# A graph network of four layers: two node stages and the attention layer's edge loop rewritten

## The reference, cut to what matters

```python
h = relu(layernorm(x)); x = x + schnet(h)     # node part: h @ w1.T goes into a table of nodes
h = relu(layernorm(x)); x = x + gat(h)        # attention layer
h = relu(layernorm(x)); x = x + mean(h)       # mean layer
h = relu(layernorm(x)); x = x + gcn(h)        # begins with h @ W1, 256 -> 64

def gat_conv(x, ...):
    h = (x @ W.T).reshape(n, 8, 32)
    logits = leaky_relu(a_s[src] + a_d[dst])
    m = segment_max(logits, dst)
    e = exp(logits - m[dst])
    return segment_sum(e / segment_sum(e, dst)[dst] * h[src], dst)

def mean(x, ...):
    return segment_sum((x @ W + b)[src], dst) / degree
```

## Time and profile before

| what | us |
|---|---|
| three runs | 5814.14, 5817.79, 5822.13 |
| median | 5817.79 |
| profiled execution | 5819.96 |
| its span, first to last instruction | 5818.2 |
| embedding | about 9 to 123 |
| attention layer's edges | about 1694 to 2965 |
| closing stage of the mean layer | about 4203 to 4337 |

### The profile page before, as it was taken

The page is one execution under the profiler, slowest core; times in us unless marked ns, Lnnn a source line. Parts: engine busy times, 40 slices in busy tenths (PEclk is TensorE's granted clock), DMA queues, the critical chain, the costliest instruction groups (busy, mean ns, idle before and its releaser), DMA issues. The chain is left out here.

```text
span 5818.2 us, 87770 instructions
## 1 busy us (share of the span) xinstructions
PE 4193.3 (72%) x24069; PEld 3457.8 (59%) x24069; DVE 3748.1 (64%) x8398; ACT 1534.4 (26%) x2511; POOL 3534.6 (61%) x3559
## 2 busy tenths in 40 slices
PE   4999999999869888888866555555563333333793
PEld 3888888888658888888855555555543333333231
DVE  4999999999548888888875444444453333333673
ACT  3766666676221111111123000000020000000570
POOL 1677777776037777777702777777627777777003
PEclk8999999999978888888887777777785555555796
DMA  5433333333334444444434333333331111111243
GB/s 164 128 102 104 103 105 103 104 103 96 95 102 110 107 107 104 106 103 102 103 106 123 105 105 105 105 105 105 108 102 32 27 27 27 27 27 27 72 113 104
DMA packets 417658, 538.48 MB, mean 93 GB/s; under 512 B 200349, under 2 KB 289577, under 8 KB 417353
## 3 DMA queue, kind: packets, MB, share of 16 engines
q0 software_dynamic: 154912, 381.74, 24.1%
q1 hardware_dynamic: 262442, 152.99, 9.8%
HBM read 482.43 MB, written 58.81 MB: 93 GB/s over the span
## 5 line engine op out<-in xcount | busy, mean ns | idle before, releaser
L1881 POOL DMA_INDIRECT l_rows<-tmp_tab,src_sb x1664 | 1576.8, 948 | 517.9 <-issue 496.3
L1994 PE MATMUL l_psa<-l_sel,l_rows 128*128 128x128 f32 (+1 forms) x4992 | 998.3, 376 | 1076.9 <-DVE l_sel L1893 819.7
L1994 PEld LDWEIGHTS l_psa<-l_sel,l_rows 128*128 128x128 f32 (+1 forms) x4992 | 878.5, 248 | 1197.5 <-DVE l_sel L1893 908.3
L1907 DVE TENSOR_TENSOR acc<-acc,l_psa 128x256 f32 (+1 forms) x1664 | 583.8, 351 | 1242.8 <-PE l_psa L1994 1076.1
L495 POOL DMA_INDIRECT l_rows<-tmp_tab,l_idx x832 | 883.7, 1062 | 373.4 <-issue 252.0
L1159 POOL DMA_INDIRECT l_rows<-tmp_tab,l_idx x832 | 891.8, 1072 | 297.3 <-issue 219.8
L793 PE MATMUL l_psw<-l_fw,l_ssp 128*128 128x256 f32 x3328 | 763.1, 382 | 0.0
L793 PEld LDWEIGHTS l_psw<-l_fw,l_ssp 128*128 128x128 f32 x3328 | 615.9, 190 | 153.7 <-issue 77.3
L1473 PE MATMUL l_psa<-l_sel,l_rows 128*128 128x128 f32 x3328 | 597.8, 308 | 33.7 <-DVE acc L1361 26.4
L1361 DVE TENSOR_TENSOR acc<-acc,l_psa 128x384 f32 x832 | 460.5, 554 | 169.2 <-issue 67.6
L1473 PEld LDWEIGHTS l_psa<-l_sel,l_rows 128*128 128x128 f32 x3328 | 501.8, 216 | 59.5 <-DVE acc L1361 36.2
(11 more groups left out here) (311 smaller groups left out, 5711.4 us busy)
## 6 DMA issues: line engine op xcount, KB each, us to landing
l_rows<-tmp_tab,l_idx POOLq DMA_INDIRECT x1664
l_edge<-in_edge_t SPq DMA_DIRECT2D x104, 256.0 KB
l_rows<-tmp_tab,src_sb POOLq DMA_INDIRECT x1664
tmp_x<-n_X SPq DMA_DIRECT2D x39, 512.0 KB
n_X<-in_x SPq DMA_DIRECT2D x26, 512.0 KB
tmp_tab<-n_O POOLq DMA_DIRECT2D x26, 512.0 KB
l_win<-tmp_att_tab SPq DMA_DIRECT2D x832, 8.0 KB
n_X<-tmp_x SPq DMA_DIRECT2D x26, 512.0 KB
```

Of the source, the lines that this page charges most:

```text
L1881: nc.gpsimd.indirect_dma_start(out=rows[g % ROWS][:, t, :], out_offset=None, in_=table[:, :], in_offset=bass.IndirectOffsetOnAxis(ap=sh["s ...
L1907: nc.vector.tensor_tensor(a, a, p, ALU.add).then_inc(added, 1)
L1994: last = nc.tensor.matmul(by_tile(g)[0:n, t, k * P:(k + 1) * P], rows[b][:, t, f:f + n], sel[b][:, t, :], start=True, stop=True)
```

## The change

In the embedding ScalarE applies the ReLU of chunk n - 1 before it copies out chunk n - 2.

In the attention layer's edges the column numbers are copied once to PSUM (`iota_ps`), and `select` reads them there. ScalarE takes the exponential of the differences twice, into `wx` for TensorE and into a PSUM area `w_ps` for VectorE; both areas share the PSUM tile `fixed`. `val_ps` moves from a tile of its own to the end of `psm`. VectorE waits for the weights ahead of the fourth select. GpSimd takes its indices straight from the tile of source numbers, with no copies, no loop and no wait for `val_done`.

The closing stage of the mean layer is new. PSUM is one tile of four quarters, and a chunk keeps one quarter: TensorE transposes the aggregate into it from `acc` directly, then the norm, the product of 64 columns, and at last the transposed table. ScalarE normalizes with a scale and a shift, VectorE makes the shift. The product with features along the partitions and its scaling are gone: the scaled table `O` is transposed (`flip`) and ScalarE copies it to `acc3` (`own_columns`). Four chunks of x are held.

```diff
@@ embed0, ScalarE
                     if at(0):
                         nm.deviations(act, at(0))
+                    if at(1):
+                        nm.relu(act, at(1), mm_done)
                     if at(2):
                         copy_out(nc, act, ph, O, psO, at(2), mm_done, stored, o_done)
-                    if at(1):
-                        nm.relu(act, at(1), mm_done)
@@ edges_gat
-        val_ps, att_ps = ph.ps("val_ps", 512)[:, 0:SH], ph.ps("att_ps", 512)[:, 0:SH]
+        att_ps = ph.ps("att_ps", 512)[:, 0:SH]
         psm = ph.ps("psm", 512)
+        val_ps = psm[:, 512 - SH:512]
+        fixed = ph.ps("fixed", 512)
+        iota_ps, w_ps = fixed[:, 0:P], fixed[:, P:P + SH]
...
+                                in_offset=bass.IndirectOffsetOnAxis(ap=sh["src_sb"][:, n * SEG + j:n * SEG + j + 1].bitcast(U32),
+                                                                    axis=0),
...
                     nc.scalar.activation(by_edge(wx[c.p])[:, :, 0:HEADS], diff[c.p][:, :].rearrange("p (t h) -> p t h", h=HEADS),
-                                         ACT.Exp).then_inc(w_done, 1)
+                                         ACT.Exp)
+                    nc.scalar.activation(w_ps, diff[c.p][:, :], ACT.Exp).then_inc(w_done, 1)
...
+                    nc.vector.tensor_tensor(sel[c.p][:, b * GT:(b + 1) * GT, :], iota_ps.unsqueeze(1).to_broadcast([P, GT, P]),
+                                            col.unsqueeze(2).to_broadcast([P, GT, P]), ALU.is_equal).then_inc(sel_done, 1)
...
+                    w = w_ps.rearrange("p (t h) -> p t h", h=HEADS)[:, part, :]
+                    nc.vector.tensor_tensor(m, m, w.unsqueeze(3).to_broadcast([P, GT, HEADS, HID]),
...
                     if a:
                         add(a, 3)
+                    if m:
+                        dve.wait_ge(w_done, m.n + 1)
                     if c:
                         select(c, 3)
@@ nodes_mean, new
+    DEEP = 4
+        ps = ph.ps("psU", DEEP * CT * D)
+        psU = [ps[:, r * CT * D:(r + 1) * CT * D] for r in range(DEEP)]
...
+        def unrolled(step):
+            for s in range(CHUNKS + 3):
+                step(*(s - j if 0 <= s - j < CHUNKS else None for j in range(4)))
...
+                for n in range(CHUNKS):
                     sp.wait_ge(x_done, n + 1)
+                    sp.dma_start(node_rows(dram["x3"], n), X[n % DEEP][:, :, :]).then_inc(x_stored[n % DEEP], 16)
+                    if n + DEEP - 1 < CHUNKS:
+                        load(n + DEEP - 1)
...
+                def own_columns(n):
+                    act.wait_ge(flipped, n + 1)
+                    nc.scalar.activation(acc3[:, n * CN:(n + 1) * CN], psU[n % DEEP][0:H3, CN:2 * CN], ACT.Copy).then_inc(copied, 1)
+                def normalize(n):
+                    act.wait_ge(shift_done, n + 1)
+                    after(act, xT_done, n - 1)
+                    for t in range(CT):
+                        last = nc.scalar.activation(norm[n % 2][:, t, :], X[n % DEEP][:, t, :], ACT.Identity,
+                                                    bias=shift[n % 2][:, t:t + 1], scale=rstd[n % 2][:, t:t + 1])
@@ nodes_mean, ScalarE
+                def step(new, mid, old, last):
+                    if old is not None:
+                        relu(old)
+                    if mid is not None:
+                        normalize(mid)
+                    if last is not None:
+                        own_columns(last)
+                    if new is not None:
+                        deviations(new)
@@ nodes_mean, VectorE
+                def step(new, mid, old, last):
+                    if mid is not None:
+                        shifts(mid)
+                    if new is not None:
+                        residual(new)
+                    if old is not None:
+                        table(old)
...
+                def back(n):
+                    after(pe, copied, n - DEEP + 1)
...
+                def flip(n):
+                    pe.wait_ge(o_done, n + 1)
+                    for t in range(CT):
+                        last = nc.tensor.transpose(psU[n % DEEP][0:H3, CN + t * P:CN + (t + 1) * P], O[n % 2][:, t, :],
+                                                   sh["ident"][:, :])
+                    last.then_inc(flipped, 1)
@@ nodes_mean, TensorE
+                def step(new, mid, old, last):
+                    if old is not None:
+                        turn(old)
+                    if new is not None:
+                        back(new)
+                    if last is not None:
+                        flip(last)
+                    if old is not None:
+                        product(old)
```

186 lines of the change are left out of this document (90 added, 96 removed).

## The result

Three runs took 5731.73, 5733.31 and 5735.03 us, median 5733.31, against 5817.79 before: 84.5 us less, a ratio of 0.9855 (0.9836 to 0.9875). The forecast was 5748, 72 less, and the range ended at 5735. So the direction and each part's sign held, and the forecast gain was too small in all three terms.

A forecast was written before the change was run, and what follows sets the result against it. Barriers make the time the sum of stages, each bound by its own limiting chain. Savings of 15.5 (embedding), 53.4 (closing stage) and 3 (attention edges), 72 us, from 5820.0 give 5748; range 5735 to 5770.

The forecast's parts named there:

- 4.60 in all: Embedding: TensorE sets the new turn, 3.56 us to the transposes plus 1.04 for them, instead of 5.99.
- 1.5 for the low clock: Closing stage of the mean layer: early turns may run at the low clock and add 1.5 us.
- the 0.3 a turn for work that doesn't mesh: Closing stage: engine sums up to 4.5 us don't mesh for nothing, so turns were taken as 4.8 us.
- Rival (b): Closing stage doesn't mesh, 6.0 us a turn, from transfers or low clock: 14 us less gain, 5762; 12 in 100.
- The steps on queues and transfers: Closing stage: loads have three turns, 14 us, to land; 246 GB/s fits under 317 at a full share.
- The median of the selects as the price of a PSUM operand: Attention edges: select from PSUM 680 ns against 684, 0.8 us less over 208; no difference taken for messages.
- The Trainium skill's figure: VectorE access overhead about 60 ns for SBUF, 125 for PSUM: 65 ns on 416 instructions, 27 us.
- The 2 us for GpSimd's relief in the fill: Attention edges: earlier start, two copies fewer and no stretched gathers bring the second chunk's values 2.0 us earlier.
- rival (c): Attention edges: VectorE's 67.1 us of issue gaps halve as GpSimd stops competing for the port: 5714; 5 in 100.
- (a): Attention edges: PSUM operands cost 34 ns on 416 VectorE instructions, so the 3 us don't come: 5765; 8 in 100.
- (d): Attention edges: banks shared by three engines make VectorE wait, slower than before; 0.25 us per instruction gives 5852; 2 in 100.
- The embedding's end of 17: Embedding: upper end of the saving, forecast at 15.5 us with ends of 11 and 17.

The follow-up runs named there:

- h3: Kernel before with GpSimd's direct gathers, message weights from PSUM with the second exponential, and VectorE's earlier wait; select still from SBUF: 5808.8 us, ratio 0.9994.
- j2: Kernel of h3 with VectorE's wait for the weights left ahead of the first message: 5814.3 us, ratio 1.0001 against the kernel before.
- g1_sel: Kernel before with GpSimd's direct gathers and the select's column numbers in PSUM, message from SBUF: 6647.6 us against 6570.7 on the slow chip, ratio 1.0104.

## Why the prediction missed by two microseconds

**The base.** 5748 is counted from the profiled execution's 5820.0. From the median, 5817.8, the same gains give 5745.9, and the same range would end at 5732.8. So the 2.2 us that the prediction left in are more than the 1.7 by which the range was missed. The forecast of the gain, 72 us instead of 84.5, is another matter, and that is what follows.

**Embedding, 15.5 forecast, 20.5 measured.** The mechanism was right; the step that failed is "3.56 us from the start of the products to the start of the transposes and 1.04 for these, 4.60 in all". 1.04 is how long the set takes to its end, and the next products start before that, 0.87 after the start of the set (75.11 to 75.99). 3.56 was measured behind idle time; without it, it is 3.45. That is 0.27 a turn, 2.7 us. The last products have no transposes ahead of them, 0.87 more, and the fill gave 1.3 (the third products at 45.68 instead of 46.97), which is scatter: kernels with the old order have them at 45.6 to 47.5. The last products themselves took 3.62 instead of 5.41, as forecast.

**Closing stage, 53.4 forecast, 55.6 measured.** Here start-to-start times had been used. To the last residual the forecast had 57.6 us for twelve turns of 4.8 and 1.5 for the low clock; it took 55.5. The turns from the fourth on alternate between 4.23 and 4.84, 4.53 on average, so the 0.3 a turn for work that doesn't mesh was the mis-sized term, 3.2 us; the 1.1 that is left for the early turns is near the 1.5. From the last residual to the last table 12.2 us went by instead of 10.9. The difference of 2.2 is no more than the old stage scatters. Rival (b), turns of 6.0 or the low clock, fell: TensorE was granted 0.92. The steps on queues and transfers held: no load waited in the steady turns.

**Attention edges, 3 forecast, 7.2 measured.** The median of the selects as the price of a PSUM operand was right: 683 ns against 684, and the message went from 1216 to 1211. The Trainium skill's figure of "Perfetto Trace Analysis", section "Optimizing Scalar/DVE Operations", by which 416 instructions would have cost 27 us more, isn't borne out here. The 2 us for GpSimd's relief in the fill were wrong in their cause: GpSimd's part alone gives 0.1, VectorE's alone 1.7 (first add 47.6 after the start), all together 2.4. The 4.8 us in the steady part weren't in the sum at all: the prediction gave VectorE's issue gaps a price only in rival (c). It also read that next to nothing of VectorE's idle time is another engine's, while its scans waited 18.1 us for TensorE; the edit left that wait as it was, so the forecast didn't suffer, but the larger gain was missed. Rival (c) had VectorE's gaps of 67.1 us halved, for the port; they fell by 7.5, and the runs show that it isn't the port: with gathers of 973 ns there are no long gaps in h3 and 16 in j2. Rivals (a) and (d) had no place: no message or select got slower, and banks shared by three engines cost nothing that shows. The Trainium skill, page "SBUF — State Buffer", section "Who interferes with whom", has VectorE with two SBUF operands contend with a GpSimd instruction that reads SBUF; the gathers' means in the table agree, step by step, on GpSimd's side.

**The range.** Its lower end was the forecast less 3.6 for turns of 4.5, 1.5 for the embedding, 4 for scatter and a little of (c). The embedding's end of 17 was the one that was too near: 4.60 was taken for a sum of two firm numbers, and 20.5 was measured. That the time lies only 1.7 us outside is no near hit: the forecast gain was 12.5 us short.

## What to carry to other kernels

The length of a turn on a pipelined engine is read from start to start between instructions that follow without idle time, never from durations that include the pipeline's end, nor from a first instruction behind a wait. A buffer more is worth the ring that it opens: here the new stage gave 55 us with four quarters of PSUM and, with its steps in nearly the same order and at a lower clock, nothing with three. Relieving an engine that waits for others gives no time, however much contention goes away, and one should look at where a loop jumps back before looking at operands: unrolling TensorE's loop gave twice what the edit of this stage did.

## What the hardware showed that I had not expected

- One chip took 6570.7 us for the kernel before where the others took 5812 to 5820. Stages of nodes were as long as elsewhere; the edge stages were longer (1422 us against 1249 from the attention layer's last add to the mean layer's first residual), with more of TensorE's waits put down to issue (341.9 us in the mean layer's edges of g1_sel, 197.8 before). On that chip the attention stage with GpSimd's gathers unrolled (and one of VectorE's edits) was 77 to 110 us slower than with its loop, where elsewhere it isn't slower. The changed kernel itself didn't run there, so whether it wins there is open.
- VectorE's gaps at two fixed places of its loop, 0.96 to 0.99 us where the others are 0.6, vanish only if one wait stands elsewhere and, in the runs made, the message reads its weights from PSUM (with the second exponential that this brings).
- A jump back in TensorE's loop costs up to 3.5 us in which it issues nothing, seven times and 22.2 us in this stage.
- In the old closing stage TensorE's clock fell for a third of some turns (mean 0.83, 9.95 us) and not of others (1.00, 8.31 us) with the same instructions. In the new stage, where TensorE hardly waits, it stayed at full speed from the fourth turn on.
